# Reading the mean itself: two layer norms without their negated mean

## What is computed

```
x = x + ln(attn(ln(x)))        # 16 heads, 4 kv heads, head size 128
x = x + ln(moe(ln(x)))         # 8 experts, top 2, and one shared expert
ln(x) = (x - mean(x)) / sqrt(var(x) + 1e-5)
attn: qkv = x @ w_qkv.T; q, k = layernorm(q, g, b), layernorm(k, g, b); rope(q), rope(k)
      causal softmax(q @ k.T / sqrt(128)) @ v, then @ w_o.T
moe:  softmax router, weights of the 2 largest renormed, silu(x @ gate) * (x @ up) @ down,
      plus sigmoid(x @ shgate) * shared expert
```

## Time and profile before

| | |
|---|---|
| the profiled execution's own time | 668.37 us |
| its span, first to last instruction | 666.4 us |
| mean granted clock of TensorE, of full speed | 0.994 |
| PE busy | 629.9 us, 95% |
| weight loads busy | 586.2 us, 88% |
| DVE busy | 553.0 us, 83% |
| ACT busy | 553.6 us, 83% |
| POOL busy | 530.0 us, 80%, 601 instructions |
| chain that ended last, by engine | PE 67%, POOL 12%, DVE 10%, ACT 5%, issue 4% |

### The profile page before, as it was taken

One profiled execution on the slowest core, in us unless ns is written; L12 is line 12 of the kernel. 1 busy time (PEld: TensorE's weight loads), 2 busy tenths in 40 slices (PEclk: granted clock), 3 DMA queues, 4 the chain that ended last, 5 costly groups with the idle time before them and its releaser, 6 DMA issues.

```text
span 666.4 us, 15665 instructions
## 1 busy us (share of the span) xinstructions
PE 629.9 (95%) x4518; PEld 586.2 (88%) x4518; DVE 553.0 (83%) x1918; ACT 553.6 (83%) x2111; POOL 530.0 (80%) x601
## 2 busy tenths in 40 slices
PE   6879999999999999999999999999799999999993
PEld 5658898999999999999999999999689889999981
DVE  4889999898899889899898999979999745555476
ACT  3589999999999999999999999999898536666643
POOL 3798898999899899989989998999877425666554
PEclk9999999999999999999999999999999999999997
DMA  8001306997650000000000000000437033444273
GB/s 333 30 0 34 104 1 196 334 335 220 4 47 0 2 1 0 2 1 1 2 1 1 1 1 2 1 1 26 144 122 228 33 100 104 128 129 121 78 254 126
DMA packets 51122, 54.27 MB, mean 81 GB/s; under 512 B 19840, under 2 KB 42752, under 8 KB 50912
## 3 DMA queue, kind: packets, MB, share of 16 engines
q1 hardware_dynamic: 47632, 43.90, 23.9%
q0 software_dynamic: 3408, 9.38, 3.8%
HBM read 23.83 MB, written 29.51 MB: 80 GB/s over the span
## 4 chain that ended last, share of the span: by engine, by line
PE 67%; POOL 12%; DVE 10%; ACT 5%; issue 4%; DMA 1%; SPq 0%; POOLq 0%; ACTq 0%; DVEq 0%
PE pQ L460 7%; PE pQ L461 7%; PE pQ L462 7%; PE pPO L460 4%; PE pPO L566 4%; PE pPO L461 4%; PE pPO L462 4%; PE pT L538 4%; PE pSS L460 3%; PE pA L460 3%; PE pA L461 2%; PE pA L462 2%; PE pSS L461 2%; POOL ropes L1993 2%; PE pSS L462 2%
## 5 line engine op out<-in xcount | busy, mean ns | idle before, releaser
L1002 ACT ACTIVATE P<-P,nmx 128x128 f32<-128x128 f32 (+1 forms) x256 | 118.8, 491 | 1.0 <-DVE nmx L1451 1.0
L460 PE MATMUL pQ<-W 128*128 128x512 f32 (+2 forms) x334 | 116.2, 348 | 2.1 <-DVE W L1365 0.8
L461 PE MATMUL pQ<-W 128*128 128x512 f32 (+2 forms) x334 | 111.6, 334 | 0.0
L462 PE MATMUL pQ<-W 128*128 128x512 f32 (+2 forms) x334 | 111.3, 333 | 0.0
L1993 POOL TENSOR_TENSOR ropes<-ropes 128x640 f32<-128x640 f32 x63 | 99.3, 1576 | 13.8 <-DVE ropes L1428 13.4
L1010 ACT ACTIVATE P<-P,rinv 128x128 f32<-128x128 f32 (+1 forms) x256 | 105.7, 481 | 2.1 <-DVE rinv L1457 2.1
L2003 POOL TENSOR_TENSOR ropes<-ropes 128x640 f32<-128x640 f32 x63 | 99.5, 1579 | 4.9
L460 PE MATMUL pPO<-W 128*128 128x256 f32 (+1 forms) x323 | 94.9, 294 | 5.6 <-DVE W L1466 3.6
L987 ACT ACTIVATE ropes<-pQ 128x128 f32<-128x128 f32 x320 | 88.5, 303 | 9.7 <-PE pQ L462 9.7
L461 PE MATMUL pPO<-W 128*128 128x256 f32 (+1 forms) x323 | 91.4, 283 | 0.0
L462 PE MATMUL pPO<-W 128*128 128x256 f32 (+1 forms) x323 | 91.2, 282 | 0.0
(11 more groups left out here) (276 smaller groups left out, 2174.5 us busy)
## 6 DMA issues: line engine op xcount, KB each, us to landing
xs<-stage SPq DMA_DIRECT2D x1, 17550.0 KB, 58.4
stage<-xs SPq DMA_DIRECT2D x39, 130.0 KB, 2.4
ropes<-in_ew SPq DMA_DIRECT2D x8, 608.0 KB, 4.9
stage<-in_wqkv SPq DMA_DIRECT2D x3, 768.0 KB, 8.9
stage<-ys SPq DMA_DIRECT2D x4, 512.0 KB, 6.5
ropes<-ys SPq DMA_DIRECT2D x4, 512.0 KB, 7.0
out<-X SPq DMA_DIRECT2D x7, 256.0 KB, 2.0
X<-in_wo SPq DMA_DIRECT2D x1, 1536.0 KB, 12.6
```

The costliest lines, as they stand in the source:

```text
L460: e.matmul(out, lh, rh, start=start, stop=False, skip_group_check=True)
L461: e.matmul(out, lh, rl, start=False, stop=False, skip_group_check=True)
L462: return e.matmul(out, ll, rh, start=False, stop=stop, skip_group_check=True)
L1002: a = e.activation(P[:, z, span(t)], P[:, z, span(t)], ACT.Exp, bias=nmx[:, z, t:t + 1], scale=-1.0, accum_out=sums[:, z, t:t + 1])
```

## The change

The tile `nm` and the two instructions that fill it go, each with its wait. `ln1_apply` and `out_scale` on POOL subtract the mean, read from `mv`, where they added the negated one, read from `nm`. The order of all other instructions is as it was.

```diff
-        nm = sb("nm", [128, 4])
@@ POOL
             def ln1_root(b):
-                e.wait_ge(s_aggr, b + 1)
-                e.tensor_scalar(nm[:, 0:2], mv[:, 0:2, 0], -1.0, None, ALU.mult)
                 root(2, mv[:, 0:2, 1], lr[:, 0:2], 1.0, (s_aggr, b + 1), s_var, s_lr, b)
@@ ln1_apply
-                    a = e.tensor_scalar(hrow[:, t, :], X[:, 2 * b + t, :], nm[:, t:t + 1], lr[:, t:t + 1], ALU.add,
+                    a = e.tensor_scalar(hrow[:, t, :], X[:, 2 * b + t, :], mv[:, t, 0:1], lr[:, t:t + 1], ALU.subtract,
                                         ALU.mult)
@@ out_scale
-                    a = e.tensor_scalar(osb[:, t, :], osb[:, t, :], nm[:, 2 + t:3 + t], lr[:, 2 + t:3 + t], ALU.add,
+                    a = e.tensor_scalar(osb[:, t, :], osb[:, t, :], mv[:, 2 + t, 0:1], lr[:, 2 + t:3 + t], ALU.subtract,
                                         ALU.mult)
@@ POOL
             def out_root(b):
-                e.wait_ge(s_oaggr, b + 1)
-                e.tensor_scalar(nm[:, 2:4], mv[:, 2:4, 0], -1.0, None, ALU.mult)
                 root(2, mv[:, 2:4, 1], lr[:, 2:4], 1.0, (s_oaggr, b + 1), s_ovar, s_olr, b)
```

## The result

The changed kernel took 674.65 us (median of 5 runs, 674.25 to 675.29) against 668.5 of the kernel before (5 runs, 668.31 to 670.64): ratio 1.0082, 95% interval 1.0070 to 1.0093. The forecast was 667.7, range 666.2 to 669.4, "same" with a chance of 0.91. It was wrong: the change costs 6 us, 0.8%, where the forecast allowed 0.5% for "same". Its profiled execution took 675.87 us with a span of 673.8, 7.4 more than the span before.

What follows compares the result with a forecast made beforehand. PE was taken as the bound from 100 to 466 us, hiding POOL's savings there; outside it 0.25 + 0.28 + 0.19 = 0.72 us came off the profiled 668.37, giving 667.7, range 666.2 to 669.4.

Steps and rivals of the forecast that it cites:

- What is exchanged.: 26 POOL tensor_scalars in ln1_apply and out_scale subtract instead of add: taken as 0, at most 1.8 us of POOL.
- Rival 5: Subtraction is slower on POOL, up to 1.8 us, mostly hidden; 0.5 in the open gives 668.9 us; chance 0.03.
- Of even 1.8 us nearly all would lie in the full stretch of PE.: Extra POOL time from a slower subtraction would fall mostly at 100 to 466 us, where PE waited once, 0.5 us.
- What is removed.: 16 instructions in ln1_root and out_root leave POOL's queue, some 0.28 us each, 4.5 us in all.
- Place by place, 120 to 410 us: 0.: Eleven of the 16 removed instructions lie where PE is full: worth 0 each, at most 3.1 us if that cover failed.
- rival 4: POOL is the bound after all: 663.9 us with all 16 on the path, 667.3 with three; chance 0.08.
- rival 3: First batch, 50.78 us: DVE loses a turn to POOL's addition, 1.4 us more, giving 669.3; chance 0.07.
- 34.9 us: 0.25.: Removed instruction at 34.9 us lets POOL's addition, DVE's WO subtraction and PE come earlier: 0.25 us gained, bounds 0 and 0.28.
- 466 us: 0.28.: Removed instruction at 466.16 us, PE run dry: POOL's addition, DVE and PE come earlier, 0.28 us gained, bounds 0 and 0.28.
- 513.57 us: 0.19.: Last out_root: the power ends sooner and out_scale(7) no longer waits, 0.19 us gained; bounds 0.19 gained, 0.5 lost.
- Rival 2: Last out_root: POOL's power keeps DVE's line 1505 out to its end, 0.45 lost instead of 0.19 gained, 668.3; chance 0.14.
- The rule weighed there: DVE and GpSimd share a port pair, locked for the full instruction; doubted for the power; by it the sum would be 0.08.

Runs made afterwards that it cites:

- e7: Kernel before with nm = +mean, subtracted instead of added in out_scale on POOL alone (12 instructions); ratio 1.0054.
- e1: Kernel before with all nm instructions kept but holding +mean, subtracted in both ln1_apply and out_scale on POOL; ratio 1.0121.
- e8: The changed kernel itself, measured again on the same chip as e5, e6 and e7; ratio 1.0077.
- e4: Kernel before without any nm instruction, additions kept, lr standing in for the mean (norms not computed rightly); ratio 1.0005.
- e11: e4 with one nm instruction kept, that of out_root(5) at 408 us; ratio 0.9991.
- e2: Changed kernel with an addition in place of the subtraction in both places (normed values not the reference's); ratio 1.0015.
- e3: Kernel before without the three nm instructions whose result POOL never uses (ln1 of batch 0, out of batches 6 and 7); ratio 1.0015.
- e9: Kernel before with nm written by DVE behind its bn_aggr instead of by POOL, one semaphore more, additions kept; ratio 1.0076.
- e5: Kernel before with an unneeded 128x320 addition tensor_scalar on POOL ahead of each of the 26 of ln1_apply and out_scale; ratio 1.0092.
- e6: Kernel before with nm = +mean, subtracted instead of added in ln1_apply on POOL alone (14 instructions); ratio 1.0033.
- e12: Kernel before with one nm instruction dropped, that of out_root(5), out_scale(5) adding lr instead; ratio 1.0015.
- e10: Kernel before with ten tensor_scalar forms timed singly on POOL at the start; subtraction cost 0.19, 0.70, 1.30 us more at 64, 256, 512 elements.

## Why the prediction was wrong, point by point

- **What is exchanged.** This step failed. It took the subtraction at 0, with an upper bound of 0.07 us each, 1.8 in all; it was 0.67 each, 17.5 in all. The 0 came from "number and shape of the operands stay", the bound from another kind of instruction, a tensor_tensor of additions. That one is not the dearest elementwise row either: tensor_tensors of the very shape, 128x256 (lines 2009 and 2157), take 729 ns, which would have made the bound 4.5 us; 1260 ns is beyond it too. The step itself said that no row showed the form; the bound did not reflect that. Rival 5 named the right mechanism, with a tenth of its size and a chance of 0.03.
- **"Of even 1.8 us nearly all would lie in the full stretch of PE."** The second failure, and what made the first one costly to the range. 1.8 in all is 0.3 a batch and may well be hidden; no run here adds so little. But a full PE covers what POOL loses only as far as POOL has pauses, 1.5 us a batch by its own waits, and not all of that (e7). The forecast asked who waits if POOL is earlier and did not ask who waits if it is later.
- **What is removed.** 0.28 us each: shown, by the 0.55 a batch between e1 and e8. POOL's count fell by 16 as said; its busy time rose.
- **Place by place, 120 to 410 us: 0.** Right for the removal from unit 14 to 46, 120 to 350 us (e4, e11 and e2 are level there to 0.1 us), and rival 4, POOL as the bound all along, falls with it. At 408 us it was wrong, see rival 3.
- **34.9 us: 0.25.** Between units 2 and 3 the delay falls by 0.27 in the changed kernel, 0.30 in e4 and 0.31 in e11, and not at all in e3, where that nm stays.
- **466 us: 0.28.** 0.27 in e3, 0.26 in the changed kernel. e11, which has both places and no lost turn, comes from 1.34 at unit 2 to 0.74 at unit 63: 0.60 gained, where the forecast had 0.53.
- **513.57 us: 0.19.** 0.27 in e3; `out_scale(7)` waits no more. Rival 2, the power that keeps DVE out to its end, is refuted by line 1505 at 1.16. The rule weighed there (the Trainium skill, SBUF — State Buffer, Who interferes with whom: an exclusive lock for the full instruction) fits the additions and the multiplication looked at here (line 1588 behind line 2003, e9's nm) and not the power.
- **Rival 3, a lost turn.** The right mechanism at the wrong place. DVE did not lose it at 50.78 but at 415.34, where the margin was 0.13 and not 0.24. It alone (1.2 to 1.4) takes back more than the forecast's sum of 0.72: with the fast form the removal comes to about 0.5 us lost (e4's delay goes from 0.86 to 1.62, less the 0.27 at 513.57, which is taken from e3). The forecast priced eleven instructions at 0 by PE's cover and looked for turns only at the other five.

In the changed kernel's 7.4 us of span: 1.7 up to unit 14, 2.7 over four batches, 2.5 at units 46 to 57, the -0.26 at 466, and 0.8 behind it, which no experiment here resolves. The 1.7 are 0.5 of a late start, the 0.27 gained and 1.5 where attention begins; e8, the same kernel started 0.7 later, is at 1.7 by unit 14 too, so start and late `hrow` share it. The half clock of 50 to 56 us lies just behind that wait. It is there in e1, e5 and e8 as well and not in e6, and they keep 0.7 of their 1.5 us against 0.6: little of the loss is the clock's. The half clock of 480 to 486 us lies in the 0.8; what it costs was not separated, and e2, e3, e11 and e12 have one near 478 without any slow form. The split of the 2.5 between POOL's bill and lost turns was not measured either. Of lost turns its trace shows one there: line 1593 at 405.50, 1.47 us long. The turn of 415 is not lost in it, line 1587 takes 0.34 at 420.30.

No kernel here beats the one before by what can be measured. The nearest that computes the reference is e3, worth about 0.5 us by its places.

## What to carry to other kernels

An exchange of one operation for another is a cost of its own until a row of that very form is seen. No other row gave a safe bound here; where there is none, time the form by itself first, as e10 does, or keep it out (negate once on two columns, then add). Before calling an engine's extra work hidden, read its own waits over a period, not only that the bound engine is full: they are the most that the cover can be worth. Read the waits of the weight loads beside those of PE. Where two engines take turns, list the turns won by a margin smaller than the shift, over the whole kernel: one instruction less cost five times its length here.

## What the hardware showed unexpectedly

- On POOL a tensor_scalar with a subtraction in either place took 1.24 to 1.25 us for 128x256, with an addition 0.55 to 0.56 (e10); the difference is 0.19, 0.70 and 1.30 at 64, 256 and 512 elements. A tensor_tensor with a subtraction took 1.71 for 128x704, no more an element than an addition.
- A DVE tensor_scalar of two elements in SBUF took 0.96 us in the mean, when its place in the queue fell beside POOL's long operations (e9, line 1487).
- Line 1588 of DVE, 128x80, took 0.24 us where it began 0.13 before POOL's addition, and 1.53 and 1.40 us where it began 0.15 and 0.26 behind its start (before, e4, e12).
